# One scan for two states, additions first in VectorE's slot, and all of an edge slot's scaling on VectorE, in a graph layer with a state-space branch

## The chip, the cores and the metric

One core of one Trainium2 chip runs the whole kernel. The metric is device microseconds of one execution, as the median of several. The engines are TensorE (PE, its weight loads PEld), VectorE (DVE), ScalarE (ACT), GpSimd (POOL, which here issues the gathers) and SyncE (SP, which issues the plain DMAs).

## What is computed

The input is a graph of 6250 nodes with 256 features and 200,000 edges sorted by target. After a layer norm, three things are made: a four-head graph attention over the edges, a Mamba branch over the nodes sorted by degree, and a gate and feed-forward on top; then a mixture of eight experts. What matters here:

```python
e = leaky_relu(s_src[src] + s_tgt[tgt], 0.2)
agg = segment_sum(proj[src] * attn[:, :, None], tgt)      # 200,000 rows of 4 x 64
dA = exp(dt[:, :, None] * A)                              # 16 states for each of 256 channels
dBx = (dt * xc)[:, :, None] * Bm[:, None, :]
h = dA_t * h + dBx_t ; y_t = h @ C_t                      # a scan over the sorted nodes
y = (y + xc * D_param) * silu(z) @ out_proj_w.T
```

## The kernel before, in words

`streams` (line 452) carries two streams at once. The **edge stream** works in "pairs", 440 of them, each the 512 edges of one chunk for one tile of 128 targets. For a pair, GpSimd gathers 4 x 128 rows of 260 floats (`gather`, L498; five pairs ahead, eight buffers of the tile el_g, freed by `summed`). ScalarE turns the target numbers into a one-hot matrix (`one_hot`, L559 and L565) and copies its transpose (`keep_turned`, L573). TensorE transposes (`turn`, L601) and spreads the targets' scores (`spread`, L613, into fl_px). Every fourth pair, VectorE computes the logits of four pairs (`logits`, a generator of five steps, L516 to L533), and ScalarE takes the exponential twice: `weights` (L577, into the last four columns of the rows) and `weights_again` (L592, into the PSUM tile fl_pw). Then the gathered rows are scaled: VectorE takes three of a pair's four columns of 256 (`scale`, L541), ScalarE the last one, head by head (`scale_last`, L584, four instructions of 64 columns). TensorE sums them into the single PSUM tile fl_ps with four matmuls (eight records in the trace) (`gather_sums`, L626), and VectorE adds that to the accumulator (`add`, L551). `gather_sums` of a pair waits for both scalings and for the addition of the pair before.

The **state stream** is Mamba: 28 chunks of 224 sorted nodes, 16 states a chunk, one state a "slot", so 448 slots; the channels are 2 x 128 (`KD` = 2). For a slot M, TensorE copies a row of B and a row of C to all partitions (`copies`, L1288, into fl_pbc, two buffers), VectorE makes dB = u * B (`inflow`, L1048), scans each half of 224 columns (`scan`, L1059, initial value from H0), and multiplies by C (`read_out`, L1068, into mb_hc). TensorE sums mb_hc over the states (`sum_up`, L1298, into fl_py). ScalarE makes dA = exp(dt * A) two slots ahead (`decay`, L1186, four buffers) and keeps the last column of a scan for the next chunk (`keep_last`, L1177). `prepare` spreads the next chunk's projections over the 16 slots by number: in slot 2 TensorE projects z, in slot 4 it runs the convolution (L1329, 32 records), in 6 and 8 the B, C and dt projections; ScalarE takes their outputs in 1, 3, 5, 7, 9 and 10 (with loads of its function table), VectorE works in 7, 8 and 10 to 12. `give_out` writes a finished chunk.

Three of four slots also carry one pair (`pair_beside`: slots with M % 4 = 1, 2, 3), so 336 pairs lie in this loop; it is unrolled over 32 slots. The other pairs run before: 36 while degrees are counted, 56 while nodes are ranked by pairwise comparison (L830), 12 while sorted rows are scattered. Each engine walks the same slot numbers in its own order, in the four functions `slot`; semaphores alone tie them. VectorE's order in a slot is: read_out(M-1), logits step, scan half 0, step, scan half 1, step, addition of pair S-3, steps, scale of pair S-1, prepare, inflow(M+1). TensorE's is: copies(M+1), which waits for read_out(M-1); sum_up(M-1); gather_sums(S-2), turn, spread; give_out; prepare. ScalarE's is: keep_last(M-1), one_hot(S+5), keep_turned(S+3), weights, give_out, prepare, decay(M+2), weights_again, scale_last(S).

## Time and profile before

| | before |
|---|---|
| median of 3 runs | 3993.34 us (3987.35 to 3993.79) |
| the profiled execution | 3986.44 us, its span 3984.8 us |
| busy, share of the span | PE 2963.8 us (74%), DVE 2733.2 (69%), ACT 2350.2 (59%), POOL 2475.2 (62%) |
| ScalarE's scaling, L584 | 1760 instructions, 463.3 us, 336 ns each |
| ScalarE's one-hot work, L559, L565, L573 | 717, 630 and 568 ns each |
| ScalarE's state copy, L1177 | 447 instructions of 182 ns |
| reading out, L1068 | 448 instructions of 612 ns |
| mean granted TensorE clock | 0.875 |

A page of the profile shows one execution. "Busy" is the time in which an engine's instructions run; an instruction's duration reaches into the start of the next, so starts tell what one occupies. A wait is told as "X <- Y": X stood idle until Y ended; "issue" is idle time in which nothing shown was waited for. The windows view gives the busy time of each engine in a stretch; the timeline gives single instructions, with the idle time before them in square brackets.

### The profile page before, as it was taken

What the parts mean: (1) busy time and instruction counts of PE and PEld (TensorE: products, weight loads), DVE (VectorE), ACT (ScalarE), POOL (GpSimd) and SP (SyncE); (2) the same over time, 40 slices, a digit from 0 to 9 for tenths busy, and PEclk for the clock granted to TensorE, in tenths of its full rate; (3) what the DMA queues carried; (4) which work ended last, traced back from release to release, by engine and by line L of the source; (5) the groups of instructions that cost most, each with busy time, mean ns of one, the idle gap of its engine ahead of it and who ended that gap; (6) DMA issues with size and microseconds to landing.
All of it is one profiled execution on the core that took longest, in us unless ns stands there. A gap on an engine that the chain in (4) does not pass through costs nothing. (4 is left out here: it accounts for less than half of the span.)

```text
span 3984.8 us, 66165 instructions
## 1 busy us (share of the span) xinstructions
PE 2963.8 (74%) x16306; PEld 2207.7 (55%) x16307; DVE 2733.2 (69%) x5474; ACT 2350.2 (59%) x5989; POOL 2475.2 (62%) x2259
## 2 busy tenths in 40 slices
PE   5355556645888878878888888788784888749998
PEld 4245445533656556556556555565562455438887
DVE  4466668953888888888888888888885688611111
ACT  2133344424887877877877877878783565512222
POOL 4488765676766766766766666666665376424443
PEclk8678777766999989998989999999997999969999
DMA  4333354455444444444444444444447233237675
GB/s 154 101 90 87 85 141 101 115 156 144 119 118 120 116 114 113 118 115 115 119 115 112 119 117 112 116 118 113 120 112 150 56 92 93 87 115 143 143 144 106
DMA packets 284702, 460.40 MB, mean 116 GB/s; under 512 B 57719, under 2 KB 203624, under 8 KB 284168
## 3 DMA queue, kind: packets, MB, share of 16 engines
q0 software_dynamic: 121472, 292.57, 30.6%
q1 hardware_dynamic: 162952, 165.07, 14.8%
q14 instruction: 220, 1.80, 0.1%
q8 instruction: 58, 0.95, 0.1%
HBM read 394.01 MB, written 63.44 MB: 115 GB/s over the span
## 5 line engine op out<-in xcount | busy, mean ns | idle before, releaser
L498 POOL DMA_INDIRECT el_g<-table,el_ix x1344 | 1377.8, 1025 | 661.0 <-issue 380.2
L626 PE MATMUL fl_ps<-el_g,el_oh 128*128 128x260 f32 x3520 | 1032.5, 444 | 319.3 <-DVE ACC L551 315.1
L626 PEld LDWEIGHTS fl_ps<-el_g,el_oh 128*128 128x128 f32 x3520 | 746.4, 220 | 647.7 <-issue 502.9
L498 POOL DMA_INDIRECT el_g<-table,eg_src x436 | 531.8, 1220 | 229.2 <-issue 128.6
L1059 DVE TENSOR_TENSOR_SCAN mb_h<-mb_dA,mb_h,mb_dB 128x224 f32<-128x224 f32 x896 | 569.5, 668 | 24.4 <-ACT mb_dA L1186 14.4
L565 ACT ACTIVATE el_oht<-el_away 128x512 bf16<-128x512 bf16 x445 | 280.3, 630 | 330.1 <-PE fl_px L613 315.7
L584 ACT ACTIVATE el_g<-el_g 128x64 f32<-128x64 f32 x1760 | 463.3, 336 | 0.0
L1298 PE MATMUL fl_py<-mb_hc,ident 128*128 128x448 f32 x896 | 432.4, 565 | 0.0
L541 DVE TENSOR_TENSOR el_g<-el_g,fl_pw 128x768 f32<-128x768 f32 x440 | 416.1, 946 | 0.0
L559 ACT ACTIVATE el_away<-el_dst,el_less 128x512 bf16<-128x512 bf16 x445 | 319.3, 717 | 152.3 <-DMA el_dst<-dst_rows 62.6
L1186 ACT ACTIVATE mb_dA<-mb_dt,mb_a 128x224 f32<-128x224 f32 x900 | 383.4, 475 | 1.4
L1048 DVE TENSOR_TENSOR mb_dB<-mb_u,fl_pbc 128x448 f32<-128x448 f32 x449 | 275.0, 612 | 130.6 <-PE fl_pbc L1288 128.7
L2176 POOL DMA_INDIRECT out<-ex_y,ex_to x112 | 174.1, 1554 | 279.5 <-DVE ex_y L2135 254.9
L1288 PE MATMUL fl_pbc<-mb_parts,mb_sel 96*128 96x224 bf16 x898 | 165.5, 267 | 203.9 <-DVE mb_hc L1068 202.3
L1068 DVE TENSOR_TENSOR mb_hc<-mb_h,fl_pbc 128x448 f32<-128x448 f32 x448 | 274.1, 612 | 18.0 <-issue 18.0
L551 DVE TENSOR_TENSOR ACC<-ACC,fl_ps 128x260 f32 x440 | 181.5, 412 | 129.9 <-PE fl_ps L626 97.1
L2135 DVE TENSOR_TENSOR ex_y<-ex_py,ex_b 128x512 f32<-128x512 f32 x56 | 38.8, 692 | 333.4 <-PE ex_py L2097 333.4
L601 PE MATMUL fl_pt<-el_ident,el_oht 128*128 128x128 bf16 x1776 | 187.2, 233 | 100.8 <-ACT el_oh L573 83.9
L601 PEld LDWEIGHTS fl_pt<-el_ident,el_oht 128*128 128x128 bf16 x1776 | 147.4, 106 | 192.3 <-ACT el_oht L565 97.4
L573 ACT CAST el_oh<-fl_pt 128x512 f32<-128x512 bf16 x443 | 251.7, 568 | 0.7
L2150 ACT COPY ex_xt<-ex_px 128x512 f32<-128x512 f32 x56 | 32.8, 585 | 345.8 <-PE ex_px L2071 345.8
L2086 PE MATMUL ex_ph<-ex_xt,ex_w 128*128 128x256 f32 x896 | 205.3, 383 | 1.8 <-DMA ex_b<-in_moe_b 1.1
(303 smaller groups left out, 5193.1 us busy)
## 6 DMA issues: line engine op xcount, KB each, us to landing
el_dst<-dst_rows SPq DMA_DIRECT2D x446, 128.0 KB, 3.5
ex_w<-in_moe_W SPq DMA_DIRECT2D x56, 512.0 KB, 3.6
el_g<-table,el_ix POOLq DMA_INDIRECT x1344
ex_x<-routed_x SPq DMA_DIRECT2D x56, 257.0 KB, 2.7
el_g<-table,eg_src POOLq DMA_INDIRECT x436
mb_x<-sorted_x SPq DMA_DIRECT2D x30, 224.0 KB, 3.2
table<-px_tr POOLq DMA_DIRECT2D x49, 130.0 KB, 2.4
px_x<-in_x SPq DMA_DIRECT2D x49, 128.0 KB, 3.4
```

The costliest lines, as they stand in the source:

```text
L498: pool.indirect_dma_start(out=G[b // GU][:, b % GU * NJ + j, :], out_offset=None, in_=dram["table"], in_offset=bass.IndirectOffsetOnAxis(a ...
L541: nc.vector.tensor_tensor(rows, rows, weight[:, at, :].unsqueeze(3).to_broadcast([P, NJ - 1, NH, FO]), ALU.mult).then_inc(s["scaled"], 1)
L559: nc.scalar.activation(AWAY[:], DST[:, n % 4, :], ACT.Abs, bias=LESS[:, 0:1]).then_inc(s["away"], 1)
L565: nc.scalar.activation(OHT[:, n % 2, :], AWAY[:], ACT.Relu, bias=1.0, scale=-1.0).then_inc(s["hot"], 1)
L584: ins = nc.scalar.activation(row[:, h * FO:(h + 1) * FO], row[:, h * FO:(h + 1) * FO], ACT.Identity, scale=row[:, D + h:D + h + 1])
L601: mm = nc.tensor.transpose(pT[:, j, :], OHT[:, n % 2, j * P:(j + 1) * P], I16[:])
L626: mm = nc.tensor.matmul(pS, OH[:, n % (2 * GU), j, :], G[n // GU % 2][:, n % GU * NJ + j, :], start=j == 0, stop=j == NJ - 1)
L1048: nc.vector.tensor_tensor(dB[:, n % 2], U[:, n // NS % 2], pBC[n % 2][:, 0, :].unsqueeze(1).to_broadcast([P, KD, TC]), ALU.mult).then_inc( ...
L1059: nc.vector.tensor_tensor_scan(H[:, n % 2, k, :], dA[:, n % 4, k, :], dB[:, n % 2, k, :], H0[:, k, n % NS:n % NS + 1], ALU.mult, ALU.add). ...
L1068: nc.vector.tensor_tensor(HC[:, n % 2], H[:, n % 2], pBC[n % 2][:, 1, :].unsqueeze(1).to_broadcast([P, KD, TC]), ALU.mult).then_inc(s["hc" ...
L1186: ins = nc.scalar.activation(dA[:, n % 4, k, :], DT[:, n // NS % 2, k, :], ACT.Exp, scale=A[:, k, n % NS:n % NS + 1])
L1298: nc.tensor.matmul(pY[:], w["ident"][:], HC[:, n % 2], start=n % NS == 0, stop=n % NS == NS - 1).then_inc(s["y"], 1)
```

## The change

Nothing but the functions below changes. Two states are now handled together ("two_states", numbered M // 2). In even slots VectorE does one scan of 2 x 2 x 225 columns: each run of 224 has a column in front, where dA is 0 and dB holds the state kept from the chunk before, so that one instruction restarts four times. In odd slots it reads out both states (896 columns), and at the slot's end makes dB of the next two states (896 columns). dB and H now have one buffer for two states in place of two for one; B and C have one PSUM tile each, two states wide. TensorE copies B in odd slots, C in even slots, and sums up two states in odd slots, behind the edge work. ScalarE keeps the last columns in odd slots, behind the one-hot work, and writes the next states into dB's front column. The addition comes first in VectorE's slot (also in the ranking stage), and the steps of `logits` follow it, one ahead of the scan or read-out and the others behind. `scale` takes four columns (1024), `scale_last` and its semaphores are gone.

```diff
+def two_states(m):
+    return Slot(m.i, m.n // 2, BODY // 2)
...
-            g, at = n // GU % 2, slice(n % GU * NJ, (n % GU + 1) * NJ - 1)
+            g, at = n // GU % 2, slice(n % GU * NJ, (n % GU + 1) * NJ)
             dve.wait_ge(s["weight"], p.of(GU) + 1)
             rows = G[g][:, at, 0:D].rearrange("p j (h f) -> p j h f", h=NH)
-            nc.vector.tensor_tensor(rows, rows, weight[:, at, :].unsqueeze(3).to_broadcast([P, NJ - 1, NH, FO]),
+            nc.vector.tensor_tensor(rows, rows, weight[:, at, :].unsqueeze(3).to_broadcast([P, NJ, NH, FO]),
                                     ALU.mult).then_inc(s["scaled"], 1)
...
-        def scale_last(act, p):
-            row = G[p.n // GU % 2][:, p.n % GU * NJ + NJ - 1, :]
-            act.wait_ge(s["row_weight"], p.of(GU) + 1)
-            for h in range(NH):
-                ins = nc.scalar.activation(row[:, h * FO:(h + 1) * FO], row[:, h * FO:(h + 1) * FO], ACT.Identity,
-                                           scale=row[:, D + h:D + h + 1])
-            ins.then_inc(s["scaled_last"], 1)
...
-            pe.wait_ge(s["scaled_last"], q + 1)
...
         def edges_vector(dve, S):
-            steps = logits(dve, S) if S.n % GU == 0 else None
-            if steps:
-                next(steps)
-                next(steps)
-                next(steps)
             add(dve, S - 3)
-            if steps:
-                next(steps)
-                next(steps)
+            if S.n % GU == 0:
+                for _ in logits(dve, S):
+                    pass
             scale(dve, S - 1)
...
-            dA = sb("mb_dA", [P, 4, KD, TC])
-            dB, H, HC = (sb(f"mb_{n}", [P, 2, KD, TC]) for n in ("dB", "h", "hc"))
+            dA = sb("mb_dA", [P, 4, KD, 1 + TC])
+            dB, H = (sb(f"mb_{n}", [P, 2, KD, 1 + TC]) for n in ("dB", "h"))
+            HC = sb("mb_hc", [P, 2, 2, KD, TC])
...
+                    dve.wait_ge(s["B"], m + 1)
+                    if not early(m, 1):
+                        dve.wait_ge(s["h"], m)
+                    wide_u = U[:, n // N2 % 2].unsqueeze(1).to_broadcast([P, 2, KD, TC])
+                    nc.vector.tensor_tensor(dB[:, :, :, 1:], wide_u, pB[:].unsqueeze(2).to_broadcast([P, 2, KD, TC]), ALU.mult
+                                            ).then_inc(s["dB"], 1)
+                def scan(p):
                     m, n = p.number, p.n
-                    if k == 0:
-                        dve.wait_ge(s["dB"], m + 1)
-                        dve.wait_ge(s["dA"], m + 1)
-                        if not early(m, 2):
-                            dve.wait_ge(s["h0"], m - 1)
-                    nc.vector.tensor_tensor_scan(H[:, n % 2, k, :], dA[:, n % 4, k, :], dB[:, n % 2, k, :],
-                                                 H0[:, k, n % NS:n % NS + 1], ALU.mult, ALU.add).then_inc(s["h"], 1)
+                    dve.wait_ge(s["dB"], m + 1)
+                    dve.wait_ge(s["dA"], 2 * m + 2)
+                    if not early(m, 1):
+                        dve.wait_ge(s["h0"], 2 * m)
+                        dve.wait_ge(s["hc"], m)
+                    line = lambda t: t.rearrange("p s k t -> p (s k t)")
+                    nc.vector.tensor_tensor_scan(line(H[:]), line(dA[:, n % 2 * 2:n % 2 * 2 + 2]), line(dB[:]), ZERO[:, 0:1],
+                                                 ALU.mult, ALU.add).then_inc(s["h"], 1)
                 def read_out(p):
                     m, n = p.number, p.n
-                    dve.wait_ge(s["h"], (m + 1) * KD)
+                    dve.wait_ge(s["h"], m + 1)
+                    dve.wait_ge(s["C"], m + 1)
                     if not early(m, 2):
                         dve.wait_ge(s["y"], m - 1)
-                    nc.vector.tensor_tensor(HC[:, n % 2], H[:, n % 2], pBC[n % 2][:, 1, :].unsqueeze(1).to_broadcast([P, KD, TC]),
-                                            ALU.mult).then_inc(s["hc"], 1)
+                    nc.vector.tensor_tensor(HC[:, n % 2], H[:, :, :, 1:], pC[:].unsqueeze(2).to_broadcast([P, 2, KD, TC]), ALU.mult
+                                            ).then_inc(s["hc"], 1)
...
                     at, b = n % NS, n // NS % 2
-                    if at == 1 and not early(c, 1):
+                    two = two_states(M)
+                    if at == 2 and not early(c, 1):
                         give_out(c - 1, 1 - b)
-                    if not early(M.number, 1):
-                        read_out(M - 1)
+                    if S:
+                        add(dve, S - 3)
                     steps = logits(dve, S) if S and S.n % GU == 0 else None
                     if steps:
                         next(steps)
-                    scan(M, 0)
+                    if at % 2:
+                        read_out(two)
+                    else:
+                        scan(two)
                     if steps:
                         next(steps)
-                    scan(M, 1)
-                    if steps:
                         next(steps)
-                    if S:
-                        add(dve, S - 3)
-                    if steps:
                         next(steps)
                         next(steps)
                     if S:
                         scale(dve, S - 1)
                     prepare(c + 1, 1 - b, at)
-                    inflow(M + 1)
+                    if at % 2:
+                        inflow(two + 1)
...
-                    nc.scalar.copy(H0[:, :, n % NS], H[:, n % 2, :, TC - 1]).then_inc(s["h0"], 1)
+                    act.wait_ge(s["h"], m + 1)
+                    nc.scalar.copy(H0[:, n % N2], H[:, :, :, TC]).then_inc(s["h0"], 1)
+                    if not early(m, N2 - 1):
+                        act.wait_ge(s["h0"], 2 * m - 2 * (N2 - 1) + 1)
+                    nc.scalar.copy(dB[:, :, :, 0], H0[:, (n + 1) % N2]).then_inc(s["h0"], 1)
...
-                        act.wait_ge(s["h"], (m - 3) * KD)
+                        act.wait_ge(s["h"], two_states(p).number - 1)
...
-                    if not early(M.number, 1):
-                        keep_last(M - 1)
                     if S:
                         one_hot(act, S + (GU + 1))
                         keep_turned(act, S + (GU - 1))
-                        if S.n % GU == 0:
-                            weights(act, S)
+                    if at % 2:
+                        keep_last(two_states(M))
+                    if S and S.n % GU == 0:
+                        weights(act, S)
                     if not early(c, 1):
                         give_out(c - 1, at)
                     prepare(c + 1, 1 - b, at)
                     decay(M + 2)
                     if S and S.n % GU == 0:
                         weights_again(act, S)
-                    if S:
-                        scale_last(act, S)
...
-                def copies(p):
+                def copies_b(p):
                     m, n = p.number, p.n
-                    if n % NS == 0:
-                        pe.wait_ge(s["bx_mid_sb"], p.of(NS) + 1)
-                        pe.wait_ge(s["bx_lo"], p.of(NS) + 1)
-                    if not early(m, 2):
-                        pe.wait_ge(s["hc"], m - 1)
+                    if n % N2 == 0:
+                        pe.wait_ge(s["bx_mid_sb"], p.of(N2) + 1)
+                        pe.wait_ge(s["bx_lo"], p.of(N2) + 1)
+                    if not early(m, 1):
+                        pe.wait_ge(s["dB"], m)
                     for r in range(2):
-                        mm = nc.tensor.matmul(pBC[n % 2][:, r, :], SEL[:, r * NS + n % NS, :], PARTS[:, n // NS % 2, :],
+                        mm = nc.tensor.matmul(pB[:, r, :], SEL[:, 2 * (n % N2) + r, :], PARTS[:, n // N2 % 2, :],
                                               start=True, stop=True, skip_group_check=True)
-                    mm.then_inc(s["BC"], 1)
+                    mm.then_inc(s["B"], 1)
+                def copies_c(p):
+                    m, n = p.number, p.n
+                    if not early(m, 1):
+                        pe.wait_ge(s["hc"], m)
+                    for r in range(2):
+                        mm = nc.tensor.matmul(pC[:, r, :], SEL[:, NS + 2 * (n % N2) + r, :], PARTS[:, n // N2 % 2, :],
+                                              start=True, stop=True, skip_group_check=True)
+                    mm.then_inc(s["C"], 1)
...
-                    copies(M + 1)
-                    if not early(M.number, 1):
-                        sum_up(M - 1)
+                    two = two_states(M)
+                    if at % 2:
+                        copies_b(two + 1)
+                    else:
+                        copies_c(two)
                     if S:
                         edges_tensor(pe, S)
+                    if at % 2 and not early(M.number, 2):
+                        sum_up(two - 1)
```

## Rows read from the trace of the kernel before

**Rows 1.** Windows, busy PE, PEld, DVE, ACT, POOL, then clock: counting, ranking, the slot loop.

```profile
200.00:560.00 360.00, 203.65 (x1615) 174.74 (x1616) 232.22 (x282) 133.07 (x354) 281.64 (x198) 0.78 0.37 100
600.00:850.00 250.00, 160.43 (x1576) 131.02 (x1575) 221.00 (x379) 110.41 (x297) 154.43 (x160) 0.72 0.44 115
986.00:3036.00 2050.00, 1667.50 (x8958) 1204.87 (x8958) 1742.63 (x3476) 1652.54 (x4424) 1385.47 (x1374) 0.93 0.46 116
```

**Rows 2.** Waits of VectorE, then of GpSimd, inside the loop (1060 to 3020 us).

```profile
DVE mb_dB L1048 <- PE fl_pbc L1288: 122.4, 67, 3.5
DVE el_s L516 <- PE fl_px L613: 51.9, 35, 2.0
DVE ACC L551 <- PE fl_ps L626: 23.7, 41, 1.2
DVE ACC L551 <- issue: 20.8, 78, 0.3
...
DVE mb_h L1059 <- ACT mb_dA L1186: 13.2, 7, 2.3
...
POOL el_g L498 <- issue: 361.6, 1159, 1.7
POOL el_g L498 <- PE fl_ps L626: 269.6, 130, 4.8
```

**Rows 3.** VectorE in order of time, two ordinary slots and the long one.

```profile
2016.21 1.25 DVE L1059 TENSOR_TENSOR_SCAN mb_h<-mb_dA,mb_h,mb_dB 128x224 f32<-128x224 f32 x2
2017.38 0.40 DVE L551 TENSOR_TENSOR ACC<-ACC,fl_ps 128x260 f32 x1
...
2019.24 0.62 DVE L1048 TENSOR_TENSOR mb_dB<-mb_u,fl_pbc 128x448 f32<-128x448 f32 x1 [0.59 <-PE fl_pbc L1288]
...
2020.31 1.25 DVE L1059 TENSOR_TENSOR_SCAN mb_h<-mb_dA,mb_h,mb_dB 128x224 f32<-128x224 f32 x2
2022.28 0.62 DVE L1048 TENSOR_TENSOR mb_dB<-mb_u,fl_pbc 128x448 f32<-128x448 f32 x1 [0.71 <-PE fl_pbc L1288]
...
2029.29 0.62 DVE L1048 TENSOR_TENSOR mb_dB<-mb_u,fl_pbc 128x448 f32<-128x448 f32 x1 [3.51 <-PE fl_pbc L1288]
...
2032.13 0.56 DVE L516 TENSOR_REDUCE el_s<-fl_px 128x128 f32<-128x384 f32 x1 [1.68 <-PE fl_px L613]
```

**Rows 4.** TensorE and ScalarE around the same long slot.

```profile
2022.84 2.43 PE L1329 MATMUL fl_pm<-mb_xt,mb_wc 128*128 128x224 f32 x12
...
2028.90 0.36 PE L1288 MATMUL fl_pbc<-mb_parts,mb_sel 96*128 96x224 bf16 x2
...
2029.86 1.92 PE L626 MATMUL fl_ps<-el_g,el_oh 128*128 128x260 f32 x8
...
2031.65 0.85 ACT L1186 ACTIVATE mb_dA<-mb_dt,mb_a 128x224 f32<-128x224 f32 x2
```

**Rows 5.** Groups of instructions of the whole span (busy us, mean ns of one, idle before).

```profile
L1059 DVE TENSOR_TENSOR_SCAN mb_h<-mb_dA,mb_h,mb_dB 128x224 f32<-128x224 f32 x896 | 569.5, 668 | 24.4 <-ACT mb_dA L1186 14.4 <-issue 10.0
...
L584 ACT ACTIVATE el_g<-el_g 128x64 f32<-128x64 f32 x1760 | 463.3, 336 | 0.0
...
L541 DVE TENSOR_TENSOR el_g<-el_g,fl_pw 128x768 f32<-128x768 f32 x440 | 416.1, 946 | 0.0
...
L1048 DVE TENSOR_TENSOR mb_dB<-mb_u,fl_pbc 128x448 f32<-128x448 f32 x449 | 275.0, 612 | 130.6 <-PE fl_pbc L1288 128.7 <-issue 0.7
...
L1660 DVE TENSOR_TENSOR_SCAN nd_inc<-nd_mask,nd_tot 128x112 f32<-128x112 f32 x7 | 2.7, 392 | 0.2
```

**Rows 6.** GpSimd in order of time in the same stretch as Rows 4: two gathers.

```profile
2021.03 1.29 POOL L498 DMA_INDIRECT el_g<-table,el_ix  x1 [0.30 <-issue]
2022.62 0.95 POOL L498 DMA_INDIRECT el_g<-table,el_ix  x1 [0.30 <-issue]
```

**Rows 7.** VectorE in order of time in the ranking stage: two dependent logit steps.

```profile
702.42 0.23 DVE L520 TENSOR_TENSOR el_z<-el_g,el_s 128x64 f32<-128x64 f32 x1
702.68 0.22 DVE L523 SCALAR_TENSOR_TENSOR el_l<-el_z 128x64 f32<-128x64 f32 x1
```

53 lines of the change are left out of this document (26 added, 27 removed).

## The prediction

> **What bounds the kernel now.** I read the stages first, then who waits for whom, then one stretch instruction by instruction. The window view [rows 1] splits the 3984.8 us span. The loop of state slots takes 2050 of them: 28 chunks of 16 slots, 73.2 us each. In it VectorE is busy 1743 us (62.2 per chunk), TensorE 1668, ScalarE 1653, GpSimd 1385. GpSimd also has 361.6 us of "issue" between gathers [rows 2], so it needs 1385 + 362 = 1747 us, as much as VectorE. No engine is full: the reader is to see two loads of 62 us per chunk in a period of 73, and to ask what the missing 11 us are. The waits of VectorE in 1960 us (26.8 chunks) of the loop [rows 2] are 122.4 us for the B and C copies from TensorE, 51.9 for the spread scores, 23.7 + 20.8 at the addition, 13.2 for the decays. GpSimd waits 269.6 us for buffers that TensorE frees, so it has 14% of slack.
>
> In order of time [rows 3], the big waits come once a chunk. TensorE runs the convolution (slot 4) from 2022.84 and only at 2028.90 copies B and C [rows 4]; VectorE waits 0.71 before it, 3.51 for these copies, then 1.68 for the spread of the next edge slot: 5.9 us a chunk, 5.9 x 26.8 = 158 of the waits. That path alternates between TensorE and VectorE. ScalarE is not on it except for its decays, ready at 2032.5 [rows 4].
>
> **The change, part by part.** A duration in a row overlaps the next instruction: two scans last 1.25, yet the addition starts 1.17 after them (2016.21 to 2017.38) [rows 3]. I subtract that 0.08 from every duration to get what an instruction occupies.
>
> *Merged scan* (224 pairs of states). Before, 4 scans = 2 x 1.17 = 2.34 us. After, one of 900 columns. Two scan rows, 668 ns for 224 columns and 392 for 112 [rows 5], give 2.46 ns a column: 0.668 + 676 x 0.00246 = 2.33 long, 2.25 occupied. From below: with the fixed part of a TENSOR_TENSOR (612 ns for 448, 946 for 768: 1.044 ns a column and 0.144 fixed) [rows 5], the short scan gives (0.392 - 0.144) / 112 = 2.21 ns, so 0.144 + 900 x 0.00221 = 2.14, 2.06 occupied. The loop's scans read their initial value from a tile and nd_inc's does not, so part of the difference between the two is fixed cost, not slope: I take 2.06. 224 x (2.34 - 2.06) = -63 us, at worst -20.
> The Trainium skill (DVE: opcode table, instruction layouts, handler registers and perf-mode slots, section 6) says the built-in scan feeds its result back to an earlier stage and runs at half throughput. At twice the 1.044 ns of a TENSOR_TENSOR column that is 2.09 ns, and the merged scan would be an estimated 2.08 us long, -76 us in place of -63. The two scan rows alone do not agree with it (2.46), unless their fixed parts differ by 42 ns.
>
> *Merged inflow and read-out*. Four of 448 columns (0.53 each) become two of 896: 0.144 + 896 x 0.001044 = 1.08, 1.00 occupied. 224 x 0.12 = -27 us.
>
> *VectorE scales four columns*. 256 more columns x 1.044 ns = 0.267 us, on 336 edge slots of the loop: +90 us.
>
> *Logit steps no longer between two scans*. Two dependent steps start 0.26 apart in the ranking stage [rows 7]; slotted in, a 0.20 us step occupied 0.12. Some 0.2 us per group of four, 84 groups: +17 us. Where no addition stands between inflow and scan (112 slots without edges), the scan waits for its predecessor to drain, 0.08: +10.
>
> So VectorE's own work in the loop goes by -63 - 27 + 90 + 17 + 10 = **+27 us**. What ScalarE gives up (four 64-column scalings a slot) and the two tiny state copies it now makes per pair, as many as before, count for nothing: VectorE hardly waits for it (13.2 us) [rows 2]. If the new scan waits for it, see below.
>
> *The waits*. Before, copies(M+1) needed the read-out of slot M's head, and the gather matmuls needed the addition that came after the scans. Now C copies need a read-out half a slot older, B copies one of two slots back, and the addition opens VectorE's slot, so TensorE's gather matmuls (1.92 us [rows 4]) begin 1.7 us sooner, the 0.53 of the read-out and the 1.17 of the scans that stood ahead of it. Outside the long slot I expect the waits of [rows 2] for copies, spreads, additions to go: 122.4 + 51.9 + 23.7 + 20.8 - 158 = 61: **-61 us**.
> In the long stretch: TensorE is busy without a break from slot 2's gather on. Counting from slot 4's head T, slot 3's gather, sum and turn end about T+0.6, then 6.1 us of convolution (2028.90 - 2022.84), so B copies come at T+7.0. VectorE does scan (2.1), addition, read-out, scaling (2.45), so it is ready at T+4.5 and waits 2.5. Slot 6's addition and logits then wait 0.8 for one gather. New: the scan of slots 6 and 7 needs slot 7's decay. ScalarE makes that after its convolution outputs and a reload of its table, ending 2.65 to 3.5 after the convolution (2032.5 - 2028.9) [rows 4], T+10.2; VectorE comes at T+9.6: 0.6. Sum 3.9 against 5.9: 28 x 2.0 = **-56 us**. The same need costs some 0.3 at slot 8, after the ping-pong over the parts: **+8**.
>
> *Before the loop*. In ranking VectorE is busy 221 of 250 us [rows 1]: 0.267 for each of 49 slots with a comparison, **+13**. In counting GpSimd is the bound (282 busy of 360 and 0.3 of issue at each of 198 gathers, 341) [rows 1]; the 0.27 x 36 = 10 us there lie under it and would show if it weren't.
>
> Sum: +27 - 61 - 56 + 8 + 13 = **-69 us**. The profiled execution took 3986.44 us, which is 6.9 below the median of 3993.34. I forecast against the median: **3924 us**, 1.7% faster. The case's own range: scan at its upper price +43, counting +10, and waits that go only half +58, hardly all at once, against 25 if the long wait shrinks to 1.5: 3899 to 4000.
>
> **Rivals.**
> *GpSimd becomes the bound.* A gather that starts inside a scan (2021.03, scan 2020.31 to 2021.56) lasts 1.29 in place of 0.95 [rows 3, 6]. The Trainium skill (GPSIMD Engine Reference, section 1) says that GpSimd's SBUF interfaces are shared with VectorE and contended by VectorE instructions with two SBUF inputs, which the scan is and inflow, read-out and scaling (one input in PSUM) are not. The trace agrees, by that row. One block of 2.06 hits a gather worse than two of 1.17: if a hit costs by the square of the length, the 0.06 x 48 = 3 us a chunk grow to 3 x (2.06 / 1.17)^2 / 2 = 4.6. GpSimd then needs 62.4 + 1.6 = 64 a chunk, and where half of its 9.6 us of buffer waits stay and the scans cost it twice as much again (3), 72: 28 x 1.2 = -34, +13: 3972. Against it: its slack is 9.6 now.
> *The coupling vanishes.* With ScalarE relieved and TensorE early, all but 1.5 us of loop turn and 2 us of the long wait goes: 63.1 + 3.5 = 66.6 a chunk, 28 x 6.6 = -185, +13: 3821. For it: TensorE and GpSimd are both below that. Against it: the convolution's 6.1 us are not split.
> *Slower: the merged scan waits for ScalarE.* One scan now needs both decays and two copies chained behind one-hot work, one slot earlier for the odd state. It decides from 69 / 224 = 0.31 us a scan on. In an ordinary slot ScalarE's one-hot work, copies and decays take some 3 us of VectorE's 3.5, so those hold. But from slot 5 it runs late, and slots 7, 9 and 10 add 0.6 to 4 us each. 1.25 us at slots 6, 8, 10 and 12 is 5 us a chunk, 140 less the 25 already counted: 3924 + 115 = 4039. For it: nothing lets the scan start in halves any more. Against: ScalarE loses 12 x 1.05 of 59 us a chunk.
> That the change does nothing can't be: every slot takes the new order.
>
> **Chances.** The forecast 0.52, GpSimd 0.14, vanishing coupling 0.15, ScalarE 0.19. A kernel's time can be told from no change at about 0.2%, 8 us. Of the forecast's 0.52, 0.49 is faster, 0.02 the same, 0.01 slower; of GpSimd's 0.10, 0.02, 0.02; the coupling 0.15 faster; of ScalarE's 0.02, 0.02, 0.15. Together 0.76, 0.06, 0.18. For 8 in 10 the range takes in the forecast's bounds and GpSimd's case, and a third of each outer one: 3845 to 4012.
>
> **What would show it.** Scan near 2.1 us, x224; inflow and read-out 1.08; scaling 1.21, x440. The wait of mb_dB falls to about 70 us, that of the addition's group (now the slot's first) to 25, mb_h waits for ScalarE some 30. The loop lasts 1965 us. GpSimd waits less than 200 us for TensorE. Wrong would be: mb_h waiting over 100 us (ScalarE), or GpSimd at under 60 us of waits, or a scan over 2.3.

## The result and the profile after

The changed kernel takes 3978.95 us, the median of 6 runs (3973.2 to 3990.91), beside 3993.9 for the kernel before in as many runs: ratio 0.9967, 95% interval 0.9955 to 0.9978. So it is faster by 0.33%, 15 us, where 69 were forecast. The rows come from one profiled execution of each kernel, and these two lie closer together: spans of 3977.9 and 3984.8 us, 6.9 apart.

Groups of the pages (busy us, mean ns of one, idle before), beside [rows 5]. The first line is the gather of the kernel before, all others are of the changed kernel:

```profile
L498 POOL DMA_INDIRECT el_g<-table,el_ix x1344 | 1377.8, 1025 | 661.0 <-issue 380.2
```

```profile
L504 POOL DMA_INDIRECT el_g<-table,el_ix x1344 | 1527.8, 1137 | 491.2 <-issue 384.2
...
L547 DVE TENSOR_TENSOR el_g<-el_g,fl_pw 128x1024 f32<-128x1024 f32 x440 | 532.2, 1209 | 0.3 <-ACT fl_pw L589 0.3
L1056 DVE TENSOR_TENSOR_SCAN mb_h<-mb_dA,mb_zero,mb_dB 128x900 f32<-128x900 f32 x224 | 468.3, 2091 | 45.2 <-ACT mb_dA L1188 22.2
...
L557 DVE TENSOR_TENSOR ACC<-ACC,fl_ps 128x260 f32 x440 | 184.6, 419 | 199.0 <-PE fl_ps L622 171.4
L1043 DVE TENSOR_TENSOR mb_dB<-mb_u,fl_pb 128x896 f32<-128x896 f32 x225 | 242.8, 1079 | 93.4 <-PE fl_pb L1288 93.4
...
L1066 DVE TENSOR_TENSOR mb_hc<-mb_h,fl_pc 128x896 f32<-128x896 f32 x224 | 241.7, 1079 | 0.2
```

The scan, the scaling and both merged multiplications last as long as forecast. The waits inside the loop (1072 to 3010 us) after, beside [rows 2]: total us, times, longest.

```profile
DVE mb_dB L1043 <- PE fl_pb L1288: 88.3, 27, 4.0
DVE ACC L557 <- PE fl_ps L622: 72.7, 102, 1.4
DVE mb_h L1056 <- ACT mb_dA L1188: 22.2, 56, 1.0
DVE mb_h L1056 <- DVE mb_dB L1043: 21.5, 75, 0.9
DVE ACC L557 <- issue: 18.6, 53, 0.6
DVE mb_y L1116 <- PE fl_py L1310: 9.6, 27, 0.5
...
DVE el_s L522 <- DMA el_g<-table,el_ix: 1.6, 2, 1.5
...
POOL el_g L504 <- issue: 368.8, 1212, 1.7
POOL el_g L504 <- PE fl_ps L622: 100.3, 77, 3.5
...
PE fl_ps L622 <- DVE ACC L557: 282.8, 141, 5.8
```

The short waits for copies and spreads went; in their place stands the addition, which opens the slot and waits for TensorE 102 times (41 times and 23.7 us before, 72.7 us now). For a gather itself (`el_s <- DMA`) VectorE waited twice, 1.6 us in all. The windows of ranking and of the loop (columns as in [rows 1]):

```profile
600.00:850.00 250.00, 170.88 (x1653) 138.67 (x1651) 235.91 (x397) 75.13 (x142) 155.58 (x164) 0.71 0.43 112
1000.00:3000.00 2000.00, 1616.07 (x8850) 1199.48 (x8851) 1728.67 (x2323) 1331.08 (x3044) 1516.83 (x1355) 0.93 0.44 117
```

VectorE's timeline cut into slots gives the balance of one chunk of 16: 72.94 us with 10.37 idle before, 72.32 with 8.99 idle after (gaps of over 0.15 us are counted). Idle time by slot, mean us:

| slot | 0 | 1 | 2 | 3 | 4 | 5 | 6 | 7 | 8 | 9 | 10 | 11 | 12 | 13 | 14 | 15 | all 16 |
|---|---|---|---|---|---|---|---|---|---|---|---|---|---|---|---|---|---|
| before | 1.52 | .26 | .15 | .34 | .71 | 3.51 | 2.06 | .30 | 0 | 0 | .02 | .38 | .41 | 0 | .71 | 0 | 10.37 |
| after | .46 | 0 | .65 | .09 | .21 | 3.28 | 1.20 | 0 | .33 | 0 | .48 | .11 | .40 | .38 | .89 | .51 | 8.99 |

The new waits have three endings. The additions of slots 10, 14 and 15 wait for TensorE's gather (0.48, 0.89 and 0.51 us). `give_out`, at the head of slot 2, waits 0.34 for TensorE's sum over the states. In slots 2 and 13 the addition stands idle 0.31 and 0.38 us on "issue", waiting for nothing that is shown.

The stretch around slots 12 to 15: TensorE and then VectorE of the changed kernel in order of time, and the windows over the same stretch:

```profile
2057.04 1.99 PE L622 MATMUL fl_ps<-el_g,el_oh 128*128 128x260 f32 x8 [0.27 <-DVE ACC L557]
...
2068.93 3.59 PE L622 MATMUL fl_ps<-el_g,el_oh 128*128 128x260 f32 x8 [5.60 <-DVE ACC L557]
...
2074.47 1.93 PE L622 MATMUL fl_ps<-el_g,el_oh 128*128 128x260 f32 x8
```

```profile
2063.14 2.09 DVE L1056 TENSOR_TENSOR_SCAN mb_h<-mb_dA,mb_zero,mb_dB 128x900 f32<-128x900 f32 x1 [0.23 <-DVE mb_dB L1043]
...
2067.38 0.63 DVE L1105 TENSOR_TENSOR mb_u<-mb_dt,mb_xc 128x448 f32<-128x448 f32 x1
2068.36 0.42 DVE L557 TENSOR_TENSOR ACC<-ACC,fl_ps 128x260 f32 x1 [0.35 <-issue]
...
2072.74 0.43 DVE L557 TENSOR_TENSOR ACC<-ACC,fl_ps 128x260 f32 x1 [0.83 <-PE fl_ps L622]
```

```profile
2058.00:2062.00 4.00, 3.15 (x19) 1.93 (x18) 3.86 (x11) 3.37 (x12) 3.23 (x5) 1.00 0.39 102
2062.00:2066.00 4.00, 0.98 (x8) 0.48 (x6) 3.58 (x4) 2.25 (x6) 3.37 (x3) 0.92 0.38 100
2066.00:2070.00 4.00, 1.07 (x3) 0.91 (x4) 3.48 (x6) 1.50 (x4) 3.10 (x3) 0.50 0.60 154
2070.00:2074.00 4.00, 4.00 (x19) 2.84 (x18) 3.17 (x4) 0.99 (x2) 1.69 (x3) 0.73 0.54 168
```

In slot 12, which has no pair, VectorE does the scan and four dt steps. TensorE has nothing but the next gather to do, and that waits for the next addition: 5.60 us idle. The granted clock stands at 0.50 by then (1.2 GHz), and the gather takes 3.59 us in place of 1.93. Slot 14's addition finds it unfinished (0.83), and slot 15's waits as well. Slot 13's own 0.35 is not TensorE's doing: the sum that its addition needs had long been ready.

Such slow gathers (of TensorE: the eight matmul records of `gather_sums` for one pair) are no novelty of the changed kernel. Counted between 1072 and 3010 us, 56 of 318 gathers took over 2.6 us before and 50 of 320 after: in slot 13 nearly always (25 of 26 chunks before, 26 of 26 after), before also in slots 1 and 6 (30 in all), after in slot 9 (19 of 27) and slot 2 (5 of 27).

### The profile page after: what moved, and what is told of

Same layout as the page of the kernel before. It is cut to its first block and busy times, and to the rows that moved or that the text cites. A ratio compares the mean times of both kernels' runs of the same rounds, so it can differ in the third digit from the quotient of the medians.

```text
span 3977.9 us, 61596 instructions
## 1 busy us (share of the span) xinstructions
PE 2936.7 (74%) x16306; PEld 2217.3 (56%) x16307; DVE 2771.0 (70%) x4357; ACT 1944.6 (49%) x4230; POOL 2643.0 (66%) x2259
## 5 line engine op out<-in xcount | busy, mean ns | idle before, releaser
L504 POOL DMA_INDIRECT el_g<-table,el_ix x1344 | 1527.8, 1137 | 491.2 <-issue 384.2
L504 POOL DMA_INDIRECT el_g<-table,eg_src x436 | 546.2, 1253 | 227.7 <-issue 130.1
L547 DVE TENSOR_TENSOR el_g<-el_g,fl_pw 128x1024 f32<-128x1024 f32 x440 | 532.2, 1209 | 0.3 <-ACT fl_pw L589 0.3
L1056 DVE TENSOR_TENSOR_SCAN mb_h<-mb_dA,mb_zero,mb_dB 128x900 f32<-128x900 f32 x224 | 468.3, 2091 | 45.2 <-ACT mb_dA L1188 22.2
L1310 PE MATMUL fl_py<-mb_hc,ident 128*128 128x448 f32 x896 | 397.7, 567 | 0.0
L1043 DVE TENSOR_TENSOR mb_dB<-mb_u,fl_pb 128x896 f32<-128x896 f32 x225 | 242.8, 1079 | 93.4 <-PE fl_pb L1288 93.4
L610 PE MATMUL fl_px<-eg_parts,el_oht 128*128 x1776 | 115.6, 177 | 180.8 <-DVE el_q L534 148.1
L1066 DVE TENSOR_TENSOR mb_hc<-mb_h,fl_pc 128x896 f32<-128x896 f32 x224 | 241.7, 1079 | 0.2
L610 PEld LDWEIGHTS fl_px<-eg_parts,el_oht 128*128 128x128 bf16 x1776 | 90.3, 100 | 204.8 <-issue 204.5
L1310 PEld LDWEIGHTS fl_py<-mb_hc,ident 128*128 128x128 f32 x896 | 155.1, 193 | 86.5 <-issue 86.5
```

The lines of the kernel that those rows point to most:

```text
L504: pool.indirect_dma_start(out=G[b // GU][:, b % GU * NJ + j, :], out_offset=None, in_=dram["table"], in_offset=bass.IndirectOffsetOnAxis(a ...
L547: nc.vector.tensor_tensor(rows, rows, weight[:, at, :].unsqueeze(3).to_broadcast([P, NJ, NH, FO]), ALU.mult).then_inc(s["scaled"], 1)
L1043: nc.vector.tensor_tensor(dB[:, :, :, 1:], wide_u, pB[:].unsqueeze(2).to_broadcast([P, 2, KD, TC]), ALU.mult).then_inc(s["dB"], 1)
L1056: nc.vector.tensor_tensor_scan(line(H[:]), line(dA[:, n % 2 * 2:n % 2 * 2 + 2]), line(dB[:]), ZERO[:, 0:1], ALU.mult, ALU.add).then_inc(s[ ...
L1310: mm = nc.tensor.matmul(pY[:], w["ident"][:], HC[:, n % 2, r], start=first and r == 0, stop=last and r == 1)
```

## The experiments

The theory after the result, A: the addition's place decides how much of TensorE's lateness VectorE sees. Rivals: GpSimd's gathers, stretched by the long scan, set the pace (G); TensorE's summing of two states ahead of a convolution or gather does (S); the work given to VectorE eats the gain (V).

The runs fell on six chips. On three of them the kernel before takes 3991 to 3994 us. On the other three (labels e1 to e8, h1, h2) it takes 4503 to 4581, though VectorE's and ScalarE's instructions last as long (the same kernel in f3 and e1: scan 669 ns, one-hot 630 ns on both); waits that no engine of the trace ends lengthen some slots by microseconds. These have their own numbers and are compared only among themselves, chip by chip: even there one and the same kernel stood at a ratio of 0.9474 (e3) on one chip and 0.966 (e6) on another. The expectations in microseconds hold for the first kind.

**The first set, on the second kind of chip.** Addition alone put first in the kernel before (e1, e7):

```diff
+                    if S:
+                        add(dve, S - 3)
                     if not early(M.number, 1):
                         read_out(M - 1)
...
-                    if S:
-                        add(dve, S - 3)
```

> The kernel before with one part of the change alone: in the loop, VectorE's addition is the first work of its slot, ahead of the read-out and the scans. Theory A (TensorE's queue order: the addition at the head waits for sums that TensorE has not finished, because its gather matmuls start late in some slots): the wait for the convolution's copies stays near 3.5 us a chunk, the waits at the addition grow from 44 us to 70 to 100, time 3985 to 4005. The forecast's own step (early additions free TensorE, the small waits go): those waits fall to under 20 us, time 3935 to 3950. Theory B (gathers stretched by long scans) changes nothing here: mean gather stays 1025 ns.

Measured: 4673.27 us, ratio to the kernel before 1.022 (95% interval 1.0193 to 1.0246, as in all brackets below): a loss of 2%, where the forecast's step promised a gain. VectorE scaling all four columns in the kernel before (e2; `scale` and `scale_last` as in the change's diff):

> The kernel before with another part alone: VectorE scales all four columns, ScalarE none. VectorE's work grows by 0.267 us x 336 = 90 in the loop and 13 in the ranking. Theory A and the forecast: most of it shows, 4060 to 4095 us, because VectorE stands on the path in ordinary slots. A theory that the chain is held by TensorE or GpSimd and VectorE has 11 us of slack a chunk says 3995 to 4020.

4579.64 us, 1.002 (1.0004 to 1.0037): some 100 us more work for VectorE cost about 8. That fits the rival that gives VectorE slack, not the 67 to 102 us above the kernel before that theory A and the forecast expected. ScalarE scaling the last column again in the changed kernel (e3, those two hunks undone):

> The changed kernel with ScalarE scaling the last column again, as before the change (pairs of states, merged scan and early addition stay). Theory A: VectorE's work falls by 90 + 13 us and at least half of it shows: 3880 to 3930. Theory C (the merged scan waits for ScalarE's decays and kept columns, so ScalarE must be relieved): mb_h waits for mb_dA over 80 us and the time is 3975 or more. Theory B (GpSimd is the bound after the change): 3960 to 3980, with POOL waiting under 60 us.

4342.9 us, 0.9474 (0.9439 to 0.9508). The changed kernel with its scan as two of 450 columns (e4):

```diff
+                    for r in range(2):
+                        ins = nc.vector.tensor_tensor_scan(line(H[:, r]), line(dA[:, n % 2 * 2 + r]), line(dB[:, r]), ZERO[:, 0:1],
+                                                           ALU.mult, ALU.add)
```

> The changed kernel with the merged scan as two instructions of 450 columns, back to back. VectorE pays 224 x 0.12 = 27 us more. Theory B (a gather that starts inside a scan waits for that scan's end, and this costs time): mean gather falls from 1137 to 1070 ns or less and the time falls by 5 to 30 us, to 3950 to 3975. Theory A: gathers may shorten, but the time goes up by 10 to 27 us, to 3989 to 4006. If the gap between two scans is too short to let a gather through, gathers stay at 1137.

4432.41 us, 0.9687 (0.9653 to 0.972). Ratios of 0.95 fitted no theory, since the changed kernel itself had stood at 0.9967, so it was run again with the next set:

> The changed kernel itself, beside the kernel before on the same chip, since the chip of the first four runs took 4571 us for the kernel before in place of 3993. If the chip is like the first one: ratio 0.9955 to 0.9978 again, 3975 to 3985 us. If it is like that of the first four runs, all engines show idle time of several us that no engine causes, and the changed kernel, with 4,569 instructions fewer, gains more: 0.93 to 0.98.

> The kernel of e3 once more (pairs, merged scan, early addition; ScalarE scales the last column). Theory A: on a chip like the first, 3880 to 3930 us, 50 to 100 below the changed kernel, since VectorE has 103 us less to do. Theory C (ScalarE late for the merged scan): 3975 or more. On a chip like that of e1 to e4: between the changed kernel and 100 us below it.

> The kernel of e1 once more (before, with the addition first and nothing else). Theory A: slower than before or equal, 3990 to 4050 us, the waits at the addition over 70 us in the loop. The forecast's step: 3935 to 3950, those waits under 20 us.

> The changed kernel with TensorE's sum over the states (sum_up, 1.6 us for two) moved from behind the edge work of odd slots to the front of even slots. Theory A (in odd slots TensorE has 3.9 us of work against VectorE's 3.5, and in slot 12 it stands idle for 5.6 us while its clock falls): the waits at the additions of slots 10, 14 and 15, 1.9 us a chunk, fall below 0.8, slot 12's idle time to 4, time 25 to 50 us less than the changed kernel. If those waits come from the clock alone (the 3.6 us gather of slot 13): slot 14's 0.9 stays, 0 to 15 us less. The wait for B after the convolution stays 3.3 a chunk in both.

On this chip (before 4502.6) the changed kernel takes 4289.88, 0.9544 (0.9498 to 0.9591); with the last column on ScalarE 4350.33, 0.966 (0.9633 to 0.9687); addition first alone 4631.97, 1.0274 (1.0246 to 1.0302); the sum moved (edit below) 4220.22, 0.9358 (0.9324 to 0.9392). So here the scaling on VectorE gains 1.2% and the moved sum 1.9% more. The size of the change's gain thus hangs on the chip: 0.3% on one kind, 4.6% on the other. That the addition alone costs 2 to 3% holds on both.

**The four again, on the first kind of chip (before 3992.02).** Summing two states at the front of the even slots (S):

```diff
+                        if not early(M.number, 1):
+                            sum_up(two - 1)
...
-                    if at % 2 and not early(M.number, 2):
-                        sum_up(two - 1)
```

> sum_up at the front of even slots, as in e8, which took the waits at slots 2 and 10 away and left those of slots 14 and 15 (0.9 + 0.5 a chunk). If those two causes are separate (TensorE's order at 2 and 10; the clock after slot 12's idle stretch at 14 and 15), a chip like the first gives 0.8 us a chunk less than the changed kernel: 3950 to 3965, ratio 0.989 to 0.993. On a chip like that of e1 to e8: ratio 0.93 to 0.95.

4009.11 us, 1.0038 (1.0024 to 1.0052): 30 us slower than the changed kernel, where 14 to 29 less were expected. The waits of slots 2 and 10 fall (0.65 to 0.30, 0.48 to 0), and no gather of slot 9 is slow any more, so these waits did come from TensorE's order. But slot 3's grow from 0.09 to 0.47, and in slot 11 VectorE now waits for the gathers themselves, 1.40 us a chunk. On this kind of chip S is thus not the cause of the lost gain: taking it away brings the next wait. Waits of this kernel in the loop:

```profile
POOL el_g L504 <- PE fl_ps L622: 72.6, 68, 2.5
...
DVE el_s L522 <- DMA el_g<-table,el_ix: 35.3, 25, 2.8
```

> Changed kernel with ScalarE scaling the last column. Theory A: VectorE has 103 us less to do, and on a chip like the first at least half shows: 3880 to 3930, ratio 0.972 to 0.985. Rival: VectorE's own work is hidden behind the alternation with TensorE, and less than 20 us shows: 3960 or more. On a chip like that of e1 to e8 stalls decide, and the ratio says little; the medians by slot should still fall by 0.27 in each edge slot.

3984.12 us, 0.9982 (0.9972 to 0.9991): level with the changed kernel (0.9955 to 0.9978; the intervals overlap), although VectorE does some 100 us less. It all comes back as waits: 12.5 us idle a chunk in place of 9.0, among them

```profile
DVE mb_dB L1054 <- PE fl_pb L1301: 110.7, 34, 4.3
DVE ACC L557 <- PE fl_ps L632: 86.8, 93, 1.7
...
DVE mb_rest L1085 <- ACT mb_parts L1224: 31.1, 27, 1.3
```

V falls on this kind of chip: giving the work back gains nothing. The rival that less than 20 us would show was right.

> The kernel before with the addition first. Theory A: no gain, 3985 to 4010, since the wait moves to the addition. The forecast's step: 3935 to 3950. On a chip like that of e1 to e8: 1.02 again.

4072.7 us, 1.0203 (1.0187 to 1.0218), 81 us slower than before. TensorE around slot 12, then VectorE:

```profile
2034.76 0.56 PE L1287 MATMUL fl_pbc<-mb_parts,mb_sel 96*128 96x224 bf16 x2 [3.40 <-DVE mb_hc L1068]
...
2036.62 3.67 PE L626 MATMUL fl_ps<-el_g,el_oh 128*128 128x260 f32 x8
```

```profile
2040.52 0.42 DVE L551 TENSOR_TENSOR ACC<-ACC,fl_ps 128x260 f32 x1 [3.27 <-PE fl_ps L626]
2040.86 0.62 DVE L1068 TENSOR_TENSOR mb_hc<-mb_h,fl_pbc 128x448 f32<-128x448 f32 x1
```

The slow gather (3.67 us) is there as in the kernel before, but the addition that needs it now stands ahead of the read-out and the scans, and TensorE's copies wait for that read-out (357 us in the loop, 193 before). Before, those instructions ran while the gather did: slot 14 waited 0.71, here 2.83, which is 59 of the 81 us.

> Changed kernel, scan in two instructions of 450. In e4 the mean gather fell to 1033 ns from 1156. Theory B (gathers held by a long scan cost time): below the changed kernel, ratio under 0.9955. Theory A (GpSimd has slack of over 100 us in the loop): 20 to 27 us above it, ratio 1.001 to 1.004.

4048.32 us, 1.0136 (1.012 to 1.0153), 69 above the changed kernel: more than either theory. 27 of these are VectorE's added work, as expected, 41 are idle time. Its gathers and GpSimd's waits:

```profile
L504 POOL DMA_INDIRECT el_g<-table,el_ix x1344 | 1395.7, 1038 | 691.6 <-issue 350.2
```

```profile
POOL el_g L504 <- PE fl_ps L622: 318.6, 215, 5.8
```

The gathers are 99 ns shorter and the kernel is slower. By itself that doesn't settle G, since something else changed too: 74 of TensorE's gather sums took over 2.6 us, 50 in the changed kernel, and the mean granted clock of the loop was 0.89 in place of 0.93. Why, is open. What speaks against G is the changed kernel's own trace: GpSimd waits 100.3 us for buffers and VectorE 1.6 us for gathers. G falls as the cause of the lost gain; it is the next bound behind it (f1).

**Where the addition belongs (before 3991.07).** Behind the scan or read-out in every slot of the loop (g1), or only in slots 10, 14 and 15 (g2). The ranking stage keeps its addition first in all of g1 to g4:

```diff
+                    late = True            # g2: at in (10, 14, 15)
+                    if S and not late:
                         add(dve, S - 3)
...
+                    if S and late:
+                        add(dve, S - 3)
```

> The changed kernel with the addition put back behind the scan or read-out in every slot of the loop; all else (pairs, four columns on VectorE) as changed. Theory A, the addition at the head is the part that costs: put ahead in the kernel before it lost 81 us, since it waits for the gather matmuls at the head of the slot instead of doing a scan meanwhile. Then this kernel gains: the waits of the addition in slots 10, 14, 15, 2 and 13 (1.8 us a chunk) fall under scan or read-out, and the gather of later slots begins about 1 us later, which costs up to 1 us in the long stretch; 3930 to 3980 against a kernel before of 3992, mean of the group's waits for fl_ps under 40 us in the loop. Theory B, GpSimd's deadline sets the time whatever VectorE's order: as late additions free the buffers later, el_s waits for DMAs in slot 11 rise over 1 us a chunk and the time is 4000 or more. Theory C, the head is worth something once states come in pairs (TensorE starts its gather before the long scan): slower than the changed kernel by 1%, about 4020.

4149.94 us, 1.0392 (1.0375 to 1.041). I had expected a gain; it loses 171 us. TensorE and VectorE in slots 2 and 3, and the windows:

```profile
2030.48 3.81 PE L622 MATMUL fl_ps<-el_g,el_oh 128*128 128x260 f32 x8 [3.82 <-DVE ACC L557]
```

```profile
2027.88 2.13 DVE L1056 TENSOR_TENSOR_SCAN mb_h<-mb_dA,mb_zero,mb_dB 128x900 f32<-128x900 f32 x1
2029.94 0.39 DVE L557 TENSOR_TENSOR ACC<-ACC,fl_ps 128x260 f32 x1
...
2034.50 0.42 DVE L557 TENSOR_TENSOR ACC<-ACC,fl_ps 128x260 f32 x1 [2.04 <-PE fl_ps L622]
```

```profile
2026.00:2030.00 4.00, 0.65 (x4) 0.12 (x2) 3.47 (x5) 2.38 (x5) 3.08 (x4) 0.86 0.59 134
2030.00:2034.00 4.00, 3.52 (x8) 2.67 (x9) 2.46 (x4) 0.00 (x0) 2.66 (x3) 0.50 0.49 132
```

Behind give_out and a scan of 2.13 us the addition comes so late that TensorE idles 3.82 us in slot 2 as well, its clock falls to 0.50, and slot 2's gather is slow in all 25 chunks counted, against 5 of 27 in the changed kernel (71 gathers of over 2.6 us between 1072 and 3010 us, against 50). Slot 3's addition waits for it, 2.9 us on average. Idle time goes from 9.0 to 14.8 us a chunk. Theory C, that the head is worth something once states come in pairs, named the right side; the loss is 4%, not 1%.

> The changed kernel with the addition behind the scan or read-out in slots 10, 14 and 15 alone, where it waits for TensorE 0.5 to 0.9 us a chunk, after slot 12 or at the end of a stretch. Theory A (place of the addition is what costs in those slots): those three waits, 1.9 us a chunk, go under the scan or read-out, 28 x 1.9 = 53 us less, near 3926 against a kernel before of 3992. Theory B (TensorE is the one that is late there, whatever VectorE does first): the wait comes back at the logits' spread or the copies of B one slot later, and the time is within 8 us of the changed kernel's 3979. Theory C (GpSimd): el_s waits for the DMA at slot 11 over 1 us a chunk and the time is 3985 or more.

3981.47 us, 0.9979 (0.9969 to 0.9989): no gain. The three waits went from 1.9 us a chunk to 0.5, and came back: at the scan behind mb_dB in slots 10 and 14 (0.21 each, which the addition had covered), in slot 0 (+0.35), in slots 2 and 3 (+0.2) and before the B copies (+0.3). Its rival B, within 8 us, was right: here the waits are TensorE's lateness, whatever VectorE does first.

> The kernel before with the merged states alone: the addition stays behind the scan or read-out, ScalarE still scales the last column. By the step between the kernels with the addition first (3.33 us a chunk... 4072.7 without pairs, 3984.1 with), pairs are worth about 80 us if their gain doesn't hang on the addition's place: 3992 - 80 = 3912. If the pairs only give back what the early addition costs (a longer wait that they hide), the gain here is small: 3980 or more. GpSimd's gathers near 1.1 us; VectorE's waits for ScalarE (mb_dA) over 60 us would say that ScalarE, with 12 x 1.05 us more a chunk, is what then limits.

4115.57 us, 1.0304 (1.0287 to 1.0321), slower than before by 125 us where 3912 was extrapolated. This is g1 with the last column on ScalarE (`scale` and `scale_last` as before the change). Slot 2's gather is slow in all 24 chunks counted (65 over 2.6 us in all).

> The changed kernel with two VectorE steps of the next chunk's dt moved one slot or two later (from 12 and 13 to 13 and 15), so that the addition of slot 12's pair (its edge slot is 13) comes sooner after the last one. In the changed kernel TensorE stands idle 5.6 us there, waiting for the addition, its granted clock falls to 0.50 and the next gather takes 3.59 us in place of 1.93. Theory A, that idle stretch and the slow gather behind it cause the waits of slots 14 and 15 (1.4 us a chunk): the idle time falls under 3 us, the gather to 2 us, and the time by some 20 to 35 us, to 3945 to 3960 against 3992. Theory B, it is off the path: the waits move to where the dt steps now stand, and the time stays within 8 us of 3979.

3963.02 us, 0.9927 (0.991 to 0.9943): the fastest version on the first kind of chip; the changed kernel wasn't on this chip, but its interval (0.9955 to 0.9978) lies wholly above. It misses its 3945 to 3960 narrowly, as its mechanism half failed: TensorE still idles 4.79 us and the gather takes 3.81, but VectorE has more to do while it runs, so slot 14's wait (0.89) is gone. Slot 13's rises from 0.38 to 0.95, so slots 12 to 15 together idle only some 0.3 us a chunk less:

```profile
2063.07 3.81 PE L622 MATMUL fl_ps<-el_g,el_oh 128*128 128x260 f32 x8 [4.79 <-DVE ACC L557]
```

**The idle stretch itself (h1, h2; second kind of chip, before 4580.98).**

```diff
+                    if at == 12:
+                        add(dve, pair_beside(M + 1) - 3)
+                    elif S and at != 13:
                         add(dve, S - 3)
```

> The changed kernel with one addition moved: that of slot 13's pair goes to the head of slot 12, which carries no pair and in which VectorE otherwise does 5 us of scan and dt work while TensorE stands idle. Theory A, what keeps the forecast gain away is that TensorE's next gather hangs on an addition that VectorE does late, and TensorE's clock has fallen by then: the idle stretch (5.6 us, clock 0.50, gather 3.59 us) goes, with it the waits of slots 12 (0.22 us, the scan behind mb_dB), 13 (0.38), 14 (0.89) and some of 15 (0.51): 1.5 to 1.9 us a chunk, 42 to 53 us, 3925 to 3937 against a kernel before of 3992. Theory B, the waits only move (as they did with the additions behind the scan in slots 10, 14 and 15): 3970 to 3985. Theory C, GpSimd: el_s waits for the DMA at slot 11 above 0.5 us a chunk.

4269.48 us, 0.9311 (0.9284 to 0.9339). The next run had four additions moved:

> The changed kernel with the additions of slots 1, 5, 9 and 13 at the heads of slots 0, 4, 8 and 12, and the register load for slot 2's addition ahead of give_out. Theory A: the gain of the kernel with slot 12 alone, and besides the pipeline's 0.2 to 0.33 us between mb_dB and the scan in slots 0, 4 and 8 and the 0.31 of issue in slot 2 go: another 0.7 to 1.0 us a chunk, 3900 to 3917 against 3992. Theory B: TensorE's long stretch (convolution, B copies at slot 5: 3.28 us) takes it back: 3925 or more. Theory C: GpSimd's gathers become the wait, el_s waits for the DMA at slot 11 over 0.5 us a chunk.

4251.73 us, 0.9273 (0.9244 to 0.9302). The changed kernel wasn't on this chip; on another of its kind it stood at 0.9544. In h1 the gather after slot 12's addition runs at once and at full speed, and the next one is late instead:

```profile
2101.67 1.99 PE L622 MATMUL fl_ps<-el_g,el_oh 128*128 128x260 f32 x8
...
2110.26 3.05 PE L622 MATMUL fl_ps<-el_g,el_oh 128*128 128x260 f32 x8 [2.55 <-DVE ACC L557]
```

The stall has moved on by one pair. Slots 12 and 13 together take 8.62 us (median) and slots 14 and 15 8.07, against 9.01 and 8.40 of the changed kernel on e5's chip: 0.7 us a chunk, 20 us, under half of the 42 to 53 expected. The whole chunk is no shorter, though: slots 9 and 10 take 11.2 us against 9.0, most of it in waits that no engine ends, and the loop's mean chunk is 80.6 us against 80.0. The two kernels ran on different chips of this kind, so no gain of h1 or h2 over the changed kernel is shown. Whether they beat g4 on the first kind of chip stays open.

## Why the prediction was wrong

Its direction was right and its size was not: 15 us for 69. The range (3845 to 4012) holds the result. Step by step, a chunk's difference times 28:

- **Work in the loop, +27**: busy time 62.57 to 63.33 us a chunk, +21. The scan takes 2091 ns and occupies 2.01 (2063.14 to 2065.15), 2.06 taken. The Trainium skill (DVE: opcode table, instruction layouts, handler registers and perf-mode slots, section 6) says that the built-in scan runs at half throughput, which gave 2.08 us as an estimate; the trace agrees.
- **Ranking, +13**: 221.00 to 235.91 busy in the same 250 us, and the loop starts 13 us later (999.1 for 986.1). That fits, though f3, whose code ahead of the loop is that of the kernel before, started its loop 8 us later as well. Slot 8, +8: 0.33 us, +9. Right.
- **The long stretch, -56**: slots 4 to 6 idle 6.28 before, 4.69 after, -45. A term was too small, the work ahead of the convolution. TensorE now sums two states there in 1.75 us, where one state's sum took 0.93, and with slot 4's head at T = 2025.71 the convolution began at T+1.4, not T+0.6. VectorE had its B copies at T+7.85, not T+7.0, and waited 3.28 us on average, not 2.5. The scan's wait for decays was 0.36, not 0.6.

```profile
2025.32 1.75 PE L1310 MATMUL fl_py<-mb_hc,ident 128*128 128x448 f32 x4
...
2027.10 2.45 PE L1342 MATMUL fl_pm<-mb_xt,mb_wc 128*128 128x224 f32 x12
```

```profile
2033.57 1.09 DVE L1043 TENSOR_TENSOR mb_dB<-mb_u,fl_pb 128x896 f32<-128x896 f32 x1 [3.10 <-PE fl_pb L1288]
```

- **The failing step: "Outside the long slot I expect the waits ... to go", -61.** They didn't: these slots idled 4.09 us a chunk before and 3.97 after, -3 us in all. Part of that hides a gain that wasn't forecast, the turns of the loop: 28 us of "issue" waits in slot 0 before, none after. Without it the waits rose by about 25.

What the runs showed in place of the failing step: the waits of slots 0, 1, 3, 7 and 11 fell by 2.1 us a chunk, and those of slots 2, 10, 13, 14 and 15 rose by 2.0. The step held that TensorE, starting its gather 1.7 us sooner, would have it done by the next addition. That is so in the slots whose waits fell. It left out three terms. The addition at the head is also the first instruction to meet a gather that is late (+1.2 us a chunk in slots 10, 14 and 15). It shows 0.3 to 0.4 us of "issue" where little stands ahead of it (+0.7 in slots 2 and 13). And `give_out` now waits for a sum that TensorE makes behind the edge work (+0.34).

The kernel before had the late gather behind slot 12 too, and paid 0.7 us for it, with the read-out and the scans running meanwhile. Its TensorE, then its VectorE:

```profile
2064.43 0.36 PE L1288 MATMUL fl_pbc<-mb_parts,mb_sel 96*128 96x224 bf16 x2 [3.79 <-DVE mb_hc L1068]
...
2066.01 3.41 PE L626 MATMUL fl_ps<-el_g,el_oh 128*128 128x260 f32 x8 [0.44 <-DVE ACC L551]
```

```profile
2069.64 0.42 DVE L551 TENSOR_TENSOR ACC<-ACC,fl_ps 128x260 f32 x1 [0.69 <-PE fl_ps L626]
```

How much of the lost gain this cover would bring back is not shown. In the kernel before, taking it away cost 59 us (f3). In the changed kernel, giving it back in the three slots where the addition waits for TensorE brought nothing (g2), and a shorter idle stretch brought 16 us (g4). So the waits that stayed are located; why TensorE and VectorE keep them between each other is open.

The five terms as measured add up to -5 us, beside 6.9 between the two profiled spans and 15 between the medians. The loop takes 2025 us, where 1965 was forecast and 2042 stood before. Two small slips in the working: the waits and the "issue" of [rows 2] cover 26.8 chunks and were used for 28, so the 61 should be 64, and GpSimd's need of 62.4 us a chunk 63.

How the parts act together, medians on three chips of the first kind, whose kernel before took 3991 to 3994:

| | addition late | addition first |
|---|---|---|
| single states, ScalarE scales the last column | 3992 (before) | 4073 (f3) |
| pairs, ScalarE scales the last column | 4116 (g3) | 3984 (f2) |
| pairs, VectorE scales all | 4150 (g1) | 3979 (the change) |

Each of the two main parts alone costs 2 to 3%, and only together do they break even. The prediction summed them as if independent. (g3 and g1 keep the ranking stage's addition first, so they stand for the loop alone.) Each part needs the other: with a scan of 2 us ahead of it, a late addition leaves TensorE idle for over 3.8 us twice a chunk; and an early one is cheap only when the read-outs and copies no longer hang on it, as the pairs arrange. That this is the whole of the interaction is argued from the timelines of slots 2, 3 and 12 to 14, not shown separately. The scaling was priced at +103 (90 in the loop, 13 in ranking). By f2 against the change it costs nothing that can be told from noise: VectorE's own work grows by that much, and its waits shrink by as much, those for ScalarE among them. With the addition late it costs 34 (g3, g1), in the kernel before about 8 (e2, second kind of chip). So adding VectorE's work to the time one for one was right only as bookkeeping of busy time: the idle time answers to it, and the sum left that out.

The rivals. GpSimd didn't become the bound, but it came near. Its gathers stretched from 1025 to 1137 ns. Over the 0.95 of an undisturbed one that is 9.0 us a chunk, where 4.6 was assumed and 3 more as the rival's worst. It now needs 68.5 us of the 72.3, and its waits other than "issue" fell from 10.0 to 3.8 a chunk (those for buffers from 269.6 to 100.3 us in the windows). The rival's sum of 72 us a chunk and its 3972 us are closer to the result than the forecast's, and that is half luck: it had the stretch right, but VectorE hardly waited for a gather.

The Trainium skill (GPSIMD Engine Reference, section 1) says that GpSimd shares its SBUF interfaces with VectorE and that VectorE instructions with two SBUF inputs contend. The trace agrees with it. The gather that starts inside this scan lasts until 0.75 us after the scan's end, the next one 0.95:

```profile
2001.41 2.09 DVE L1056 TENSOR_TENSOR_SCAN mb_h<-mb_dA,mb_zero,mb_dB 128x900 f32<-128x900 f32 x1
...
2001.66 2.59 POOL L504 DMA_INDIRECT el_g<-table,el_ix  x1 [3.28 <-PE fl_ps L622]
...
2004.56 0.95 POOL L504 DMA_INDIRECT el_g<-table,el_ix  x1 [0.30 <-issue]
```

The coupling didn't vanish, and the merged scan waited for ScalarE 22 us only, 0.1 a scan. Of what was to show it, durations, the scan's wait (30 said, 22 seen) and GpSimd's (under 200, 100 seen) came true; the mb_dB wait (88 for 70) and the addition's (91 with its issue part, for 25) did not.

## What to carry to other kernels

Before an instruction that waits is moved to the head of a slot, look for the one slot in which its producer is late, and count what stood in front of it there as cover: in the kernel before that cover was worth 59 us (f3). Parts that touch the same ring (here addition, gather, scaling) are not priced one by one: try the two-by-two table, since two losses can make a draw. An idle stretch of TensorE can cost twice, once by itself and once by the slower matmuls after it, and moving work about often only hands it to the next turn of the ring (f1, g2, h1). When a forecast adds an engine's work and subtracts its waits, ask what the waits will do when the work changes: here they took nearly all of it back (f2).

## What the runs showed of the hardware

- A gather that starts inside a VectorE scan is held until the scan is done. Of 246 that started inside one of the changed kernel's scans (2.09 us), 223 ended 0.7 to 0.8 us after that scan's end, where an undisturbed one takes 0.95 in all; the other 23 had started in its first 0.1 us and took 0.95. With two scans of 450 columns back to back (1142 ns each, f4) they ended so after the first of the two, and the mean fell from 1137 to 1038 ns.
- After 3.4 to 5.6 us without work for TensorE, in the rows shown of the kernel before, the change, f3, g1 and g4, the same eight matmul records took 3.4 to 3.8 us in place of 1.93; in the windows of the change, f3 and g1 TensorE's granted clock was at 0.50 (1.2 GHz). A shorter gap can do it too, and not each time: in slot 9 of the changed kernel TensorE stood idle 1.25 us in nearly every chunk, and 19 of 27 gathers behind it took over 3 us, at a mean granted clock of 0.53 to 0.63, while 8 took 1.99 at full clock.
- Three of six chips ran the kernel before 13 to 15% slower with VectorE's and ScalarE's instructions as long, and the changed kernel, seen on one of the three, only about 7.8% slower (4289.88 against 3978.95). The cause was not found.
- Back-to-back dependent instructions left 0.21 to 0.23 us between mb_dB and the scan, which an addition in between covers.
